# A four-layer conv and mixture-of-experts kernel: the wide layers' preparations issued tile by tile in the other half's expert stage, and their loops written out

## The chip, the cores and the metric

The kernel runs on one core of a Trainium2 chip. The metric is device time in microseconds. TensorE (PE) does the matmuls, VectorE (DVE), ScalarE (ACT) and GpSimd (POOL) the rest, SyncE (SP) issues plain DMAs and GpSimd the indirect ones. Each engine runs its own queue of instructions in order and waits on semaphores that other engines and DMAs raise.

## The reference

The input is 16 images of 64 channels and 24 x 24 pixels. Four blocks follow each other; each is a "conv" part and a "ffn" part, both added to their input:

```python
for l in range(4):
    x = x + conv[l](layernorm_over_channels(x))       # eps 1e-6
    t = tokens(x)                                      # 9216 tokens of 64
    t = t + ffn[l](layernorm(t))                       # eps 1e-5
    x = images(t)
# conv[0]: gate from the matrix square root (5 Newton-Schulz steps) of each image's covariance
# conv[1]: max over 2 of a*x + b, a and b from the pooled image;  conv[2]: gate from Haar band means
# conv[3]: 3 x 3 depthwise convolution and bias
# ffn[0], ffn[1]: 8 experts, 64 -> 128 (256) -> 64 with gelu and biases, the 2 best per token, weighted
# ffn[2], ffn[3]:
probs = softmax(flat @ router.T); p, idx = top_k(probs, 2); p = p / (p.sum() + 1e-9)
y = (silu(flat @ w1[e].T) * (flat @ w3[e].T)) @ w2[e].T     # 64 -> 682 -> 64, 8 experts
out = sum over the token's two experts of p * y
```

## The kernel before, in words

The images are worked on in two halves of 8 images, 4608 tokens each: `x[h]` holds 36 blocks of 128 tokens. Layers 0 and 1 are "narrow": every token goes through all 8 experts (`dense`), in slots of 512 tokens times one chunk of an expert, with the gates as factors. Layers 2 and 3 are "wide": tokens are sorted by expert. The order of the whole program is written by hand, each engine's queue for itself.

`prep(l, h)` is a half's preparation for a layer: layer norm (`ln`), the conv part, layer norm, routing (`route`). It is a generator with numbered steps (LN1, CONV, LN2, ROUTE), one on each engine; `Woven(prep(...)).upto(stage)` issues steps up to a number. In the narrow layers `dense` gets the other half's next preparation as `aside` and issues a few steps after each slot, by the plan of `weave`. For the wide layers the order is: `Woven(prep(2, 1)).upto(LAST)` alone, `moe(2, 0)`, `moe(2, 1)`, then `prep(3, 0)` and `prep(3, 1)` alone, the rounding of layer 3's weights (`wprep`), `moe(3, 0)`, `moe(3, 1)`, and the two last sums.

`moe(l, h)` is the expert stage of a half: 44 tiles (`TILES`) of 256 rows, 4 to a loop body (`UNROLL`), so 11 bodies (`LOOPS`); the first and the last are written out and the nine in between are a loop on each engine (`middle`). A tile's experts come from a packed word that TensorE loads per body (`experts`). Per tile TensorE transposes the rows of the tile after next (`turn_rows`, L1549, into banks 6 and 7 in turn), and for each of three groups (g) of hidden units does `up23` (8 matmuls, L1563 and L1564) and the last tile's `down23` (L1577, L1579). ScalarE does SiLU (`silu`, L753), a rounding (`high`, L761) and the copy of the transposed rows (`take`, L769, L770). DVE does `product` (L1189), `low` (L1193) and one `evict` (L1180) per tile.

Rows travel through DRAM. When `route` has the positions (`pos_ready`), GpSimd sends each of 36 blocks twice to its sorted places (`scatter`, `send`, L564, 72 indirect DMAs a half, reading `rowsb`). SyncE loads sorted tiles (L491) once all sends of the half have landed. GpSimd returns each finished tile with two indirect DMAs (`back`, L586) to token order; SyncE brings these back (`bring`, L523), and DVE's `combine` (L840 to L844) adds them to `x`. GpSimd's `back(l, 0, scatter(l, 1))` spreads the 72 sends of the second half over the 44 tiles of the first half's stage; `back(l, 1, ...)` has none beside it, and the sends of `scatter(3, 0)` follow the stages of layer 2 and lie beside `prep(3, 1)`.

SyncE loads the wide layers' weights in five pieces (`load_stage`, L479), ScalarE and DVE split each into two 16-bit parts. The expert output bias of the narrow layers is added on TensorE by two matmuls per unit with one row each (L1514). `conv0` forms each image's column sums (L1332) and covariance (L1340) image by image.

## Time and profile before

| | us |
|---|---|
| median of 3 runs | 2542.31 (2541.0 to 2554.62) |
| profiled execution | 2537.53 |
| its span, first to last instruction | 2535.7 |

| engine | busy us | share of the span |
|---|---|---|
| PE | 1678.8 | 66% |
| DVE | 1733.9 | 68% |
| ACT | 1347.7 | 53% |
| POOL | 980.1 | 39% |

The mean granted clock of TensorE is 0.778 of full speed. Times within the span are counted from its start. Busy times of an engine sum its instructions, which overlap a little on DVE and ACT. "Idle before" a row is the time in which the engine did nothing ahead of it, with what ended it; "issue" is a wait that nothing in the profile explains, "remote" one ended by no instruction that the profile could name.

### The profile page before, as it was taken

Reading aid. Unit: us, or ns where it says so; the run is one execution under the profiler, and the core shown is the slowest. Engines: PE = TensorE matmul, PEld = TensorE weight load, DVE = VectorE, ACT = ScalarE, POOL = GpSimd, SP = SyncE. Lnnn points to the kernel's source line nnn. Section 1 sums busy time; section 2 is a strip of 40 time slices with the busy share of each in tenths; the row PEclk is TensorE's granted clock in tenths of the full one; section 3 lists DMA queues with packets and bytes.
Section 4 is the critical chain, followed back from the end, with each engine's and each line's share of the span. In section 5 each row is a group of like instructions: output and inputs, shape, how many; then the busy total and the mean of one; then the engine's idle time right before and its main releaser. Section 6 shows DMA issues by size and latency. Waiting matters only on the chain.

```text
span 2535.7 us, 52266 instructions
## 1 busy us (share of the span) xinstructions
PE 1678.8 (66%) x17212; PEld 1245.9 (49%) x17213; DVE 1733.9 (68%) x2890; ACT 1347.7 (53%) x2453; POOL 980.1 (39%) x955
## 2 busy tenths in 40 slices
PE   4387787787867776537766679951221777777995
PEld 4253443453434433326666568840111666666884
DVE  3668668768775874566555568888775655556888
ACT  1356556777786677425445467740002544445774
POOL 1034334322231248404554534430481444553553
PEclk7587767878885879758788789975555877788998
DMA  6000000000020000000000020010002000002002
GB/s 276 22 2 1 23 1 1 1 2 1 2 85 5 1 9 21 15 4 26 25 24 23 17 65 26 27 66 0 12 22 78 26 24 23 24 18 63 27 27 82
DMA packets 52976, 75.98 MB, mean 30 GB/s; under 512 B 14873, under 2 KB 37610, under 8 KB 50174
## 3 DMA queue, kind: packets, MB, share of 16 engines
q1 hardware_dynamic: 30626, 43.26, 5.3%
q0 software_dynamic: 22208, 30.81, 3.5%
q8 instruction: 91, 1.49, 0.3%
q14 instruction: 51, 0.42, 0.1%
HBM read 40.89 MB, written 35.19 MB: 30 GB/s over the span
## 4 chain that ended last, share of the span: by engine, by line
PE 32%; DVE 14%; issue 7%; POOL 4%; ACT 4%; another core or an unknown queue 4%; DMA 1%; ACTq 0%; POOLq 0%; SPq 0%; DVEq 0%
PE bank L1563 11%; PE bank L1564 10%; PE bank L1577 4%; POOL rows L564 3%; DVE tmp L1030 2%; PE bank L1579 2%; POOL x L599 1%; DVE hb L1189 1%; ACT hl L761 1%; DVE act L1189 1%; PE bank L1459 1%; PE bank L1322 1%; ACT act L753 1%; ACT hb L753 1%
## 5 line engine op out<-in xcount | busy, mean ns | idle before, releaser
L586 POOL DMA_INDIRECT y<-ysb,ids x352 | 394.3, 1120 | 563.6 <-DVE ysb L1180 475.1
L599 POOL TENSOR_TENSOR x<-x,ysb 128x256 f32<-128x256 f32 x288 | 268.7, 933 | 668.6 <-DVE ysb L1258 660.6
L1563 PE MATMUL bank<-xT,gA 128*114 128x256 f16 x1056 | 342.3, 324 | 156.2 <-issue 51.3
L736 ACT ACTIVATE hb<-bank,bias_sb 128x512 f32<-128x512 f32 x432 | 298.8, 692 | 245.1 <-issue 137.1
L564 POOL DMA_INDIRECT rows<-rowsb,pos x288 | 305.4, 1060 | 293.8 <-DVE pos L1132 211.9
L1189 DVE TENSOR_TENSOR act<-bank,act 114x512 f32<-114x512 f32 x352 | 242.8, 690 | 236.5 <-ACT act L753 159.4
L753 ACT ACTIVATE act<-bank 114x512 f32<-114x512 f32 x352 | 210.2, 597 | 308.7 <-PE bank L1564 240.8
L1564 PE MATMUL bank<-xT,gB 128*114 128x256 f16 x1056 | 311.5, 295 | 0.0
L1563 PE MATMUL bank<-xT,uA 128*114 128x256 f16 x1056 | 311.2, 295 | 0.0
L1564 PE MATMUL bank<-xT,uB 128*114 128x256 f16 x1056 | 310.8, 294 | 0.0
L1577 PE MATMUL bank<-dW,hl 114*128 x2112 | 279.3, 230 | 32.2 <-issue 22.4
L1579 PE MATMUL bank<-dW,hl 114*128 x2112 | 260.8, 201 | 13.6 <-issue 13.3
L1563 PEld LDWEIGHTS bank<-xT,gA 128*114 x1056 | 148.6, 141 | 206.1 <-issue 194.2
L1193 DVE TENSOR_TENSOR hl<-act,hl 114x512 f16<-114x512 f32 x352 | 240.4, 683 | 0.0
L1577 PEld LDWEIGHTS bank<-dW,hl 114*128 114x128 f16 x2112 | 199.7, 103 | 59.5 <-issue 46.3
L761 ACT ACTIVATE hl<-act 114x512 f16<-114x512 f32 x352 | 220.6, 627 | 0.0
L1189 DVE TENSOR_TENSOR hb<-bank,hb 114x512 f32<-114x512 f32 x176 | 121.6, 691 | 131.9 <-ACT hb L753 96.2
L1579 PEld LDWEIGHTS bank<-dW,hl 114*128 114x128 f16 x2112 | 199.6, 103 | 16.6 <-issue 12.0
L1249 DVE TENSOR_TENSOR act<-hb,act 128x512 f16<-128x512 f32 x216 | 165.8, 768 | 49.0 <-ACT act L736 46.1
L1503 PE MATMUL bank<-rowsb,w 128*128 128x512 f16 x432 | 194.1, 449 | 6.2 <-DVE w0d L1238 6.2
L1249 DVE TENSOR_TENSOR hl<-hb,hl 128x512 f16<-128x512 f32 x216 | 159.3, 738 | 55.4 <-ACT hl L736 52.5
L1504 PE MATMUL bank<-rowsb,w 128*128 128x512 f16 x432 | 195.2, 452 | 0.0
(239 smaller groups left out, 3457.6 us busy)
## 6 DMA issues: line engine op xcount, KB each, us to landing
xs<-rows SPq DMA_DIRECT2D x176, 65.0 KB
stage<-up SPq DMA_DIRECT2D x8, 1368.0 KB, 6.1
rows<-land POOLq DMA_DIRECT2D x8, 1137.5 KB, 18.4
y<-ysb,ids POOLq DMA_INDIRECT x352
rows<-rowsb,pos POOLq DMA_INDIRECT x288
stage<-down SPq DMA_DIRECT2D x2, 1368.0 KB
rowsb<-y SPq DMA_DIRECT2D x4, 640.0 KB, 5.9
rows<-land POOLq DMA_DIRECT2D x4, 585.0 KB, 20.5
```

What stands on the lines that cost most here:

```text
L564: pool.indirect_dma_start(rows_d[l - SPARSE][h], bass.IndirectOffsetOnAxis(pos[h][:, k, j:j + 1], 0), words(h)[:, j * RW // 2:(j + 1) * RW ...
L586: pool.indirect_dma_start(y_d[h], bass.IndirectOffsetOnAxis(ids[h][:, t * SUB + u:t * SUB + u + 1], 0), ysb[t % UNROLL][:, u * C:(u + 1) * ...
L599: pool.tensor_tensor(xv, xv, tg[u % 2], ALU.add).then_inc(s["added"], 1)
L736: ins = a.activation(dst[:, 0:SPAN * P], PB[w % 3][:, :], ACT.Gelu, scale=1.0 / WSCALE, bias=b1T[l][:, at:at + 1])
L753: a.activation(hold(k, g)[0:CH, :], PB[q % 2][0:CH, :], ACT.Silu, scale=1.0 / WSCALE).then_inc(s["s_ready"], 1)
L761: a.activation(hl[g][0:CH, 0:2 * ROWS], hold(k, g)[0:CH, :], ACT.Copy).then_inc(s["hi_ready"], 1)
L1189: v.tensor_tensor(p, PB[2 + q % 2][0:CH, :], p, ALU.mult).then_inc(s["prod_ready"], 1)
L1249: v.tensor_tensor(p[:, SPAN * P:2 * SPAN * P], hid[w % 2][:, 0:SPAN * P], p[:, 0:SPAN * P], ALU.subtract).then_inc(s["lo_ready"], 1)
L1563: pe.matmul(PB[bank][0:CH, o], w[0][:, at], xT[k][:, :], start=True, stop=False)
L1564: ins = pe.matmul(PB[bank][0:CH, o], w[1][:, at], xT[k][:, :], start=False, stop=True)
L1577: pe.matmul(y[:, o:o + 2 * C], hl[g][0:CH, col:col + P], w, start=(g == 0 and c == 0 and u == 0), stop=False, skip_group_check=True)
L1579: ins = pe.matmul(y[:, o:o + C], hl[g][0:CH, 2 * ROWS + col:2 * ROWS + col + P], w[:, 0:C], start=False, stop=(g == G - 1 and c == 1), ski ...
```

## The change

Loops: `JOIN` and `middle` go; all 11 bodies of each stage are written out on TensorE, ScalarE and DVE (SyncE keeps its loop). Preparations: `moe` takes an `aside`, and after each of its 132 slots (44 tiles x 3) issues steps by the plan of `inner(l, h)`. `prep(2, 1)` is issued in `moe(2, 0)` from tile 1, `prep(3, 0)` in `moe(2, 1)` and `prep(3, 1)` in `moe(3, 0)` from tile 5, each over 48 slots (`INNER` 16 tiles); the combine of layer 3's first half is issued in `moe(3, 1)` from tile 5. Sends: GpSimd starts the sends beside a stage a tile before that plan ends (`inner_end`) and spreads the 72 over the tiles left; `scatter(3, 0)` now lies beside `back(2, 1)`. Banks: the transposed rows use bank 6 alone, since bank 7 (`BP`) serves the preparations. Narrow layers: the bias matmuls become one with two rows per unit (`b2p`, its second row moved there by a DMA), and `conv0` works on pairs of images with 128 columns.

```diff
-JOIN = 1
+INNER = 16
...
+            sp.wait_ge(s["stage_used"], 1)
+            sp.dma_start(b2p[1:2, :], b2[:, 2 * E * C:4 * E * C]).then_inc(s["b2_moved"], 16)
...
+        NSLOT = TILES * G
+
+        def inner(l, h):
+
+            if (l, h) == (NL - 1, 1):
+                todo, begin, over = [LN1 + k / 4 for k in range(8)], 5 * G, 8 * G
+            else:
+                l2 = (n_of(l, h) + 1) // HALVES
+                todo, begin, over = stages(l2), (G if l2 == SPARSE else 5 * G), INNER * G
+            return [-1] * begin + [todo[min(len(todo), -(-(v + 1) * len(todo) // over)) - 1] for v in range(NSLOT - begin)]
+
+        def inner_end(l, h):
+
+            plan = inner(l, h)
+            return plan.index(plan[-1]) // G
...
             def back(l, h, aside):
 
-                todo = TOPK * NT
+                todo, begin = TOPK * NT, inner_end(l, h) - 1
+                left = TILES - begin
                 for t in range(TILES):
-                    for _ in range((t + 1) * todo // TILES - t * todo // TILES):
+                    k = t - begin
+                    for _ in range((k + 1) * todo // left - k * todo // left if k >= 0 else 0):
                         next(aside, None)
...
                 back(l, 0, scatter(l, 1))
-                back(l, 1, iter(()))
-                if l + 1 < NL:
-                    first = scatter(l + 1, 0)
+                first = scatter(l + 1, 0) if l + 1 < NL else iter(())
+                back(l, 1, first)
...
-                    a.activation(xT[r][:, :], PB[6 + r % 2][:, :].bitcast(FP16)[:, 0:ROWS], ACT.Copy
+                    a.activation(xT[r][:, :], PB[6][:, :].bitcast(FP16)[:, 0:ROWS], ACT.Copy
                                  ).then_inc(s["xT_done"], 1)
...
-            Woven(prep(2, 1)).upto(LAST)
             for h in range(HALVES):
-                moe(2, h)
-            for h in range(HALVES):
-                Woven(prep(3, h)).upto(LAST)
+                moe(2, h, Woven(after(2, h)))
             Woven(wprep()).upto(LAST)
             for h in range(HALVES):
-                moe(3, h)
-            for h in range(HALVES):
-                for p in range(NP):
-                    combine(NL - 1, h, p)
+                moe(3, h, Woven(after(3, h)))
+            Woven(joined(NL - 1, 1)).upto(LAST)
...
-                        for i, b in enumerate((b2h[l], b2l[l])):
-                            row = b[:, e * C:(e + 1) * C].unsqueeze(1).broadcast_to([1, SPAN, C])
-                            pe.matmul(y[:, 0:SPAN * C], one16[0:1, :], row, start=(i == 0), stop=False, skip_group_check=True)
+                        row = b2p[:, (l * E + e) * C:(l * E + e + 1) * C].unsqueeze(1).broadcast_to([2, SPAN, C])
+                        pe.matmul(y[:, 0:SPAN * C], one16[0:2, :], row, start=True, stop=False, skip_group_check=True)
...
-                    if t == 0 or isinstance(i, int):
-                        wait_from(pe, s["xT_done"], i * UNROLL + (tb + k + t - 1))
-                    bank = PB[6 + r % 2][:, :].bitcast(FP16)
+                    wait_from(pe, s["xT_done"], i * UNROLL + (tb + k + t))
+                    bank = PB[6][:, :].bitcast(FP16)
...
+                            aside.upto(plan[(i * UNROLL + k) * G + g])
...
-                pe.wait_ge(s["route_ready"], 2 * (l + 1))
+                pe.wait_ge(s["route_ready"], n_of(l, h) + 1)
+                if (l, h) == (SPARSE, 0):
+                    pe.wait_ge(s["gated"], unit_base(SPARSE, 0))
                 turn_rows(0, 0, 0)
                 turn_rows(0, 1, 0)
-                body23(0, first=True)
-                middle(pe, body23)
-                body23(LOOPS - 1, last=True)
+                for i in range(LOOPS):
+                    body23(i, i == 0, i == LOOPS - 1)
+                aside.upto(LAST)
```

## Rows read from the trace of the kernel before

**Rows 1.** Busy time by stretch: start:end, length, PE, PEld, DVE, ACT, POOL, clock, DMA.

```profile
0.00:1048.00 1048.00, 749.76 (x8118) 424.78 (x8119) 718.61 (x1234) 657.62 (x1000) 352.94 (x381) 0.78 0.08 28
1048.00:1133.00 85.00, 27.09 (x114) 23.21 (x114) 56.42 (x110) 13.91 (x18) 1.66 (x2) 0.50 0.01 2
1133.00:1462.00 329.00, 230.45 (x2196) 207.56 (x2196) 182.37 (x308) 161.77 (x352) 160.46 (x156) 0.81 0.08 23
1462.00:1682.00 220.00, 193.46 (x2200) 171.25 (x2200) 182.31 (x309) 159.40 (x352) 103.97 (x90) 0.97 0.12 36
1682.00:1806.00 124.00, 24.01 (x92) 17.41 (x92) 97.78 (x148) 10.50 (x11) 6.77 (x6) 0.50 0.08 31
1806.00:1928.00 122.00, 24.02 (x92) 17.42 (x92) 96.28 (x148) 15.25 (x13) 84.42 (x73) 0.50 0.07 20
1928.00:1960.00 32.00, 0.31 (x4) 0.32 (x4) 14.88 (x5) 7.73 (x3) 0.00 (x0) 0.50 0.38 140
1960.00:2290.00 330.00, 236.08 (x2199) 211.83 (x2197) 181.93 (x308) 161.84 (x353) 160.43 (x156) 0.80 0.08 23
2290.00:2509.00 219.00, 193.52 (x2200) 172.16 (x2200) 181.52 (x307) 159.64 (x352) 104.46 (x89) 0.97 0.12 36
2509.00:2536.00 27.00, 0.05 (x2) 0.00 (x0) 21.79 (x17) 0.00 (x0) 4.95 (x4) 0.54 0.49 175
```

**Rows 2.** Timeline of DVE in layer 2's expert stages: start, us, line, tile.

```profile
1224.69 0.42 DVE L1180 TENSOR_REDUCE ysb<-bank 128x128 f32<-128x256 f32 x1
...
1393.31 0.42 DVE L1180 TENSOR_REDUCE ysb<-bank 128x128 f32<-128x256 f32 x1
...
1473.43 0.69 DVE L1189 TENSOR_TENSOR act<-bank,act 114x512 f32<-114x512 f32 x1 [12.32 <-ACT act L753]
...
1535.91 0.42 DVE L1180 TENSOR_REDUCE ysb<-bank 128x128 f32<-128x256 f32 x1
...
1639.67 0.42 DVE L1180 TENSOR_REDUCE ysb<-bank 128x128 f32<-128x256 f32 x1
```

**Rows 3.** Groups of GpSimd by line, 1133 to 1462 us: count, busy, mean ns, idle before.

```profile
L586 POOL DMA_INDIRECT y<-ysb,ids x85 | 89.9, 1058 | 149.5 <-DVE ysb L1180 120.2 <-issue 29.3
L564 POOL DMA_INDIRECT rows<-rowsb,pos x69 | 70.1, 1015 | 21.0 <-issue 20.7 <-POOL rowsb L572 0.3
```

**Rows 4.** Timeline of a run of GpSimd's calls and of TensorE and ScalarE beside it.

```profile
1434.50 0.27 PE L1564 MATMUL bank<-xT,uB 128*114 128x256 f16 x1
...
1435.10 1.01 POOL L586 DMA_INDIRECT y<-ysb,ids  x1 [0.30 <-issue]
...
1438.99 0.96 POOL L564 DMA_INDIRECT rows<-rowsb,pos  x1 [0.30 <-issue]
...
1441.37 0.60 ACT L753 ACTIVATE hb<-bank 114x512 f32<-114x512 f32 x1 [5.76 <-remote]
```

**Rows 5.** Waits of ScalarE, 1133:1460 (two rows) and 1465:1684: total, times, longest.

```profile
ACT hb L753 <- remote: 41.7, 9, 6.6
ACT act L753 <- remote: 22.8, 9, 5.3
...
ACT act L753 <- PE bank L1564: 37.8, 77, 2.4
```

**Rows 6.** Timeline of DVE in layer 1's second half: slots 1, 61 and 85.

```profile
766.96 0.69 DVE L1249 TENSOR_TENSOR hl<-hb,hl 128x512 f16<-128x512 f32 x1 [1.73 <-ACT hl L736]
...
913.76 0.69 DVE L1249 TENSOR_TENSOR hl<-hb,hl 128x512 f16<-128x512 f32 x1 [0.45 <-ACT hl L736]
...
946.33 0.68 DVE L1249 TENSOR_TENSOR hl<-hb,hl 128x512 f16<-128x512 f32 x1
```

**Rows 7.** Timeline of DVE in the tail: its wait for the second half's return.

```profile
2521.48 1.23 DVE L840 SCALAR_TENSOR_TENSOR rowsb<-rowsb,gts 128x1024 f32<-128x1024 f32 x1 [1.12 <-DMA xn<-y]
```

**Rows 8.** Timeline of SyncE after layer 2: loads of layer 3's weights.

```profile
1697.20 236.65 SPq L479 DMA_DIRECT2D stage<-up  x3
```

**Rows 9.** Timeline around a tile's start: ScalarE's copy, TensorE's first matmul.

```profile
1406.50 0.38 ACT L770 ACTIVATE xT<-bank 128x256 f16<-128x256 f16 x1
...
1407.04 0.31 PE L1563 MATMUL bank<-xT,gA 128*114 128x256 f16 x1 [0.70 <-DVE act L1189]
```

**Rows 10.** TensorE's bias matmuls of the narrow layers (line L1514), ns min/median/max.

```profile
L1514 PE MATMUL bank<-land,one x576: 267/278/416, 121.6 to 1043.7; 1*128 1x256 f16 x192
```

**Rows 11.** Timeline of DVE in the first layer: its wait for the column sums.

```profile
28.43 0.68 DVE L919 COPY gx<-bank 1x512 f32<-1x512 f32 x1 [7.04 <-PE bank L1332]
```

More of the change, by code:

```diff
@@ L378, in stages @@
         def stages(l):
-            return ([LN1 + k for k in range(10)] + [CONV + k for k in range(CONV_STEPS[l])] + [LN2 + k for k in range(10)]
+            first = [LN1 + k / 4 for k in range(8)] + [LN1 + k for k in range(2, 10)]
+            return ((first if l > SPARSE else [LN1 + k for k in range(10)]) + [CONV + k for k in range(CONV_STEPS[l])] + [LN2 + k for k in range(10)]
                     + [ROUTE + k for k in range(26)])
@@ L403, in experts @@
             return {k: eng.snap((w >> (3 * (k + 1))) & (E - 1), min_val=0, max_val=E - 1) for k in tiles}
-        def middle(eng, body):
-            with eng.Fori(0, (LOOPS - 2) // JOIN) as i:
-                for j in range(JOIN):
-                    body(i * JOIN + (j + 1))
         def split_base(l, h):
@@ L784, in body @@
                                 take(i, k, 2)
+                            aside.upto(plan[(i * UNROLL + k) * G + g])
                     if last:
                         high(i, UNROLL - 1, G - 1)
+                if (l, h) == (SPARSE, 0):
+                    a.wait_ge(s["down_ps"], slot_base(1, 1) + len(slots(1)))
                 take(0, 0, 0)
                 take(0, 1, 0)
-                body(0, first=True)
-                middle(a, body)
-                body(LOOPS - 1, last=True)
+                for i in range(LOOPS):
+                    body(i, i == 0, i == LOOPS - 1)
+                aside.upto(LAST)
             def after(l, h):
+                if (l, h) == (NL - 1, 1):
+                    return
                 yield from prep(*divmod(n_of(l, h) + 1, HALVES))
@@ L1207, in body23 @@
                                 low(i - 1, UNROLL - 1, G - 1)
-                            if k >= 2:
+                            if g == 0 and k >= 2:
                                 evict(i, k - 2)
-                            elif not first:
+                            elif g == 0 and not first:
                                 evict(i - 1, k + UNROLL - 2)
-                body23(0, first=True)
-                middle(v, body23)
-                body23(LOOPS - 1)
+                            aside.upto(plan[(i * UNROLL + k) * G + g])
+                if (l, h) == (SPARSE, 0):
+                    v.wait_ge(s["added"], unit_base(SPARSE, 0))
+                for i in range(LOOPS):
+                    body23(i, i == 0)
+                aside.upto(LAST)
                 low(LOOPS - 1, UNROLL - 1, G - 1)
@@ L1267, in dense, with joined @@
                 aside.upto(LAST)
+            def joined(l, h):
+                for p in range(NP):
+                    yield LN1 + p
+                    yield from combine(l, h, p)
             def after(l, h):
+                if (l, h) == (NL - 1, 1):
+                    yield from joined(NL - 1, 0)
+                    return
                 yield from prep(*divmod(n_of(l, h) + 1, HALVES))
@@ L1328, in conv0 @@
                 pe.wait_ge(s["mixed_ready"], turn(s["mixed_ready"]))
-                for smp in range(HB):
-                    ops = pieces(*divmod(smp, QS))
-                    for i, o in enumerate(ops):
-                        ins = pe.matmul(BP[0:1, smp * C:(smp + 1) * C], onef[:, 0:1], o, start=(i == 0), stop=(i == 4))
+                for s4 in range(QS):
+                    for i, o in enumerate(pieces(s4)):
+                        ins = pe.matmul(BP[0:1, s4 * P:(s4 + 1) * P], onef[:, 0:1], o, start=(i == 0), stop=(i == 4))
                 ins.then_inc(s["sums_ps"], 1)
@@ L1335, in conv0 @@
                 pe.wait_ge(s["rows_ready"], turn(s["rows_ready"]))
-                for smp in range(HB):
-                    q, s4 = divmod(smp, QS)
-                    ops = pieces(q, s4)
-                    for i, o in enumerate(ops):
-                        pe.matmul(BP[q * C:(q + 1) * C, s4 * C:(s4 + 1) * C], o, o, start=(i == 0 and s4 == 0),
-                                  stop=False, skip_group_check=True)
-                for smp in range(HB):
-                    q, s4 = divmod(smp, QS)
-                    ins = pe.matmul(BP[q * C:(q + 1) * C, s4 * C:(s4 + 1) * C], srow[0:1, 1, smp * C:(smp + 1) * C],
-                                    srow[0:1, 0, smp * C:(smp + 1) * C], start=False, stop=True, skip_group_check=True)
+                for s4 in range(QS):
+                    o4 = slice(s4 * P, (s4 + 1) * P)
+                    for i, o in enumerate(pieces(s4)):
+                        pe.matmul(BP[:, o4], o, o, start=(i == 0), stop=False, skip_group_check=True)
+                    ins = pe.matmul(BP[:, o4], srow[0:1, 1, o4], srow[0:1, 0, o4], start=False, stop=True, skip_group_check=True)
                 ins.then_inc(s["cov_ps"], 1)
@@ L1594, in body23 @@
                                 down23(i - 1, UNROLL - 1, g, es[-1])
+                            aside.upto(plan[(i * UNROLL + k) * G + g])
                     if last:
@@ L1618, in after @@
             def after(l, h):
+                if (l, h) == (NL - 1, 1):
+                    return
                 yield from prep(*divmod(n_of(l, h) + 1, HALVES))
@@ L1628, in _ @@
                     dense(l, h, Woven(after(l, h)))
[L1629 to L1637 removed]
+            for l in range(SPARSE, NL):
+                pe.wait_ge(s["w_lo"], (l - SPARSE + 1) * PIECES)
+                for h in range(HALVES):
+                    moe(l, h, Woven(after(l, h)))
 def kernel(**inputs):
```

56 lines of the change are left out of this document (28 added, 28 removed).

## The prediction

> **What bounds the kernel now.** I read three views in this order: busy time by stretch, the DVE's evictions (one per tile of 256 rows) and the waits of ScalarE. The stretches [rows 1] cut the 2535.7 us span into the two narrow layers (0 to 1048), the preparation of layer 2's second half (85 us), the expert stages of layer 2 (329 and 220 us), both preparations of layer 3 (124 and 122 us), the rounding of its weights (32 us), its expert stages (330 and 219 us) and 27 us of tail. Two things are to be seen.
>
> First, the three bare preparations (331 us) and the tail leave TensorE almost unused, but not VectorE: it is busy for 56.4 of 85, 97.8 of 124 and 96.3 of 122 us. A second-half expert stage has DVE busy for 182.3 of 220 us, of which 12.32 us are the wait at its start [rows 2], so about 88% while tiles run. What is woven into an expert stage goes onto an engine that is nearly full there.
>
> Second, the same 44 tiles take 110 us more in a first half than in a second half, at 0.81 granted clock against 0.97. From tile 12 to tile 34 one takes (1393.31 - 1224.69) / 22 = 7.66 us in the first half and (1639.67 - 1535.91) / 22 = 4.72 us in the second [rows 2]. All that differs is GpSimd's queue: in a first half it has, beside two returns per tile (L586), the 72 + 72 / 44 = 1.64 sends per tile (L564) of the other half's rows, about 1.3 us each with the 0.30 us before them [rows 3]. GpSimd is only 49% busy, so its own time isn't the bound. What I see is TensorE's signals held back while GpSimd issues many calls in a row: the last matmul of a group (L1564) starts at 1434.50, GpSimd issues without a gap until 1439.95, and ScalarE's SiLU on that bank (L753) starts at 1441.37 after 5.76 us of idle time [rows 4]. Such waits come to 64.5 us in the first half; in the second, where calls come in twos, the longest of ScalarE's waits for that bank is 2.4 us [rows 5]. So a first half is bound by runs of GpSimd calls; a second half by DVE, with TensorE close behind.
>
> A rule speaks against that reading: the Trainium skill, page "SBUF — State Buffer", section "Who interferes with whom", says that PE and ACT never wait on anyone. The wait in this trace, 5.76 us, disagrees; what would follow if the rule held here is the first rival.
>
> **The change part by part.** Sums are against the profiled execution (2537.5 us, span 2535.7).
>
> *Sends.* The number of sends is the same, 144 per layer, but the 72 of layer 3's first half leave the bare preparation after it (84.4 us of GpSimd in 1806 to 1928 [rows 1], which cost nothing there) and enter the second expert stage of layer 2. So three expert stages carry them, not two. They are also denser: GpSimd starts them only a tile before the woven preparation ends, tile 15 of 44 in layer 2's first stage (72 sends in 29 tiles, 2.5 each) and tile 19 in the next two (72 in 25, 2.9 each). A tile then has 4.5 to 4.9 GpSimd calls in a row. Price: the first half of now pays 7.66 - 4.72 = 2.94 us per tile for 1.64 sends, 1.8 us per send by these rows, and by the stages 329 - 220 plus 8 us of shorter start = 117 us per 72 sends, 1.6 us each. In denser runs the start of a run, which isn't held, is shared: a tile of 4.1 us unheld work plus 0.9 us of landing plus 1.3 us for each call past the second gives 8.2 to 8.7 us, or 9.0 to 9.6 where two tiles' runs join, so 8.6 and 9.1 us; minus 4.72, that is 112 us a stage. Three stages 336 against 234 now: **+102**. Bounds: GpSimd's own time as the only limit (4.5 and 4.9 calls of 1.3 us, 5.8 and 6.4 us a tile: 31 + 2 x 42 = 115 in all, -119), and 1.8 us for each send (389, +155).
>
> *Preparations.* Each is issued in slots (three a tile), one or two steps after each slot's own work, over 16 tiles from tile 1 or tile 5. Nearest row: layer 1's second half, where layer 2's first preparation is woven into the first 65 slots. Its first 60 slots take 913.76 - 766.96 = 146.8 us, the 24 after them 32.6, 1.36 us each [rows 6]: weaving costs 146.8 - 60 x 1.36 = 65 us for work that stands bare at 85, though DVE has far more room there. Beside experts DVE is at 88%, so the floor is DVE's own time: 56.4 less some 8 us idle in 16 tiles for layer 2, 97 less 8 for layer 3. Above it come steps in which TensorE waits in order for DVE and DVE for TensorE. I take 78 us for layer 2's (bare 85: -7) and 114 for each of layer 3's (bare 124 and 122: -18). Bounds 48 to 90 and 88 to 140. The last two tiles of each lie beside sends, when DVE idles anyway: -6 and twice -10. Together **-51**. Behind the steps queue, on DVE the next product, on TensorE the next gate matmuls, on ScalarE the next SiLU; that is why I don't go to the floor.
>
> *Combine.* The sums of layer 3's first half, 11 us of DVE at 2509, go beside tiles of the last stage. The tail doesn't shorten, since DVE then waits for the second half's return at 2521.48 [rows 7] in any case. DVE in that stage gets 10.6 us more: **+7** (0 to +11).
>
> *Weights of layer 3.* SyncE's second load waits behind the return of layer 2's second half; it was issued at 1697.20 and done in the shade of a preparation [rows 8]. Now no preparation stands between, and the 32 us stretch begins with that return, about 6 us of returns and 6 of load: **+12** (+5 to +20).
>
> *One bank for transposed rows.* Bank 7 goes to the preparations, so the transposes of the tile after next wait for ScalarE's copy of the next one. TensorE starts a tile at 1407.04 when the product is there; the copy before runs at 1406.50 for 0.38 us [rows 9]. The transposes used to fit into the wait ahead; now they follow the copy, 0.2 to 0.4 us a tile where nothing else is late, the 44 tiles of the last stage and some 10 others: **+15** (0 to +50).
>
> *Loops written out.* The load of the expert word remains. Tiles inside a body take about 0.2 us less than the mean of 4.72, so a turn costs 0.8 us, nine per stage, and only the last stage runs unhindered: **-5** (0 to -30, all 36 turns). The Trainium skill, page "Runtime: NRT & Kernel Launch", section "Instruction fetch mechanics", says that a taken branch out of the current pages stalls for a fetch, while straight code is fetched ahead. By that rule the whole -30 would come; where a stage is held by GpSimd or DVE, a turn has nothing to give back.
>
> *Narrow layers.* One bias matmul per unit goes (288 of 576, 0.28 us each, overlapped [rows 10]), on TensorE's path only where it is last; DVE's wait for TensorE's column sums in the first layer (7.04 us [rows 11]) and the like shorten by 1 or 2 us, twice; a 2 us wait for the moved bias row is added at 118 us. TensorE is busy for 750 of 1048 us there: **-16** (0 to -40).
>
> Sum: +102 - 51 + 7 + 12 + 15 - 5 - 16 = **+64**, span 2600, time 2602; the median of the runs lies 4.8 us over the profiled execution, so **2605 us**.
>
> **The rivals.** *GpSimd's runs don't hold TensorE* when they are sends only or regular, as the sends issued back to back from 1806 to 1928 didn't lengthen that preparation (122 against 124 us [rows 1]). Against: the first half's tiles [rows 2]. Then sends cost 115 in all, not 336: 2605 - 221 = 2384. (The Trainium skill's rule of the SBUF page above would have this result.) *Weaving at the floor*: DVE never waits, and the bank costs nothing: preparations 48 and twice 88, combined -56 more, -15 for the bank, -10 elsewhere: about 2520. For: 88% in [rows 1]. Against: [rows 6]. *Sends at the full price*: 1.8 us for each (+53), and no shade for a preparation's last tiles (+26), because joined runs hold TensorE while DVE waits for it: about 2684, slower than now. It decides once a run of calls outlasts the work that lies ready, as ten calls of two joined tiles would (13 us). *The change hides nothing because steps pile up*: if GpSimd's wait for the positions at tile 15 or 19 blocks its returns, DVE's evictions stop four tiles later; I give it little, since the positions come in the same tile by the plan.
>
> **How the numbers follow.** Chances: my forecast (2550 to 2645) 0.42, full price (2645 to 2710) 0.13, weaving at the floor (2480 to 2550) 0.24, unheld TensorE (2330 to 2480) 0.17, piled-up steps (above 2710) 0.04. The range 2450 to 2680 holds about 8 in 10; the forecast's own is 2550 to 2645. A measurement of this kernel tells about 0.5% (13 us) from no change: faster 0.36, same 0.09, slower 0.55.
>
> **What would show it.** In the changed profile: the second stage of layer 2 at some 430 us with 72 sends in it, last tiles at 8.5 to 9.5 us with long ScalarE waits beside runs of five GpSimd calls, and a granted clock near 0.8; tiles with preparation at 9 (layer 2) and 11 to 12 us (layer 3) with DVE at 85% or more; the last stage at 225 to 235 us. I am wrong if tiles beside sends take 6 to 7 us, or if a woven preparation of layer 3 adds under 95 us.

## The result, and the profile after

The changed kernel takes 2650.07 us (median of 4 runs, 2647.22 to 2650.71), the kernel before beside it 2541.65 us: a ratio of 1.0427 (95% interval 1.0401 to 1.0452). It is slower by 108 us. The forecast was 2605 us, in a range from 2450 to 2680. The profiled execution took 2647.22 us with a span of 2645.3 us, against 2535.7 before, so 109.6 us have to be found.

Busy time by stretch, after (start:end, length, PE, PEld, DVE, ACT, POOL, clock, DMA). These answer to [rows 1]: the narrow layers; first stage of layer 2 with its preparation and then with sends; second stage, plain, with preparation, with sends; weights; the same three parts of layer 3's first stage; the last stage; the tail.

```profile
0.00:1041.00 1041.00, 708.77 (x7656) 411.71 (x7656) 720.33 (x1236) 655.69 (x1000) 352.27 (x381) 0.79 0.08 28
1041.00:1230.00 189.00, 124.24 (x1030) 114.75 (x1029) 129.26 (x236) 90.14 (x172) 40.09 (x36) 0.75 0.05 15
1230.00:1454.00 224.00, 145.28 (x1282) 129.41 (x1280) 108.03 (x183) 93.71 (x203) 120.91 (x121) 0.75 0.08 23
1454.00:1507.00 53.00, 33.76 (x316) 29.32 (x317) 34.62 (x51) 24.54 (x55) 15.10 (x15) 0.76 0.21 68
1507.00:1712.00 205.00, 119.12 (x933) 109.58 (x932) 155.15 (x258) 77.93 (x150) 44.49 (x41) 0.70 0.05 12
1712.00:1900.00 188.00, 119.86 (x1047) 106.26 (x1045) 88.11 (x149) 75.72 (x164) 106.14 (x107) 0.74 0.08 23
1900.00:1957.00 57.00, 5.02 (x24) 4.10 (x25) 16.08 (x6) 14.29 (x11) 9.22 (x8) 0.50 0.39 150
1957.00:1995.00 38.00, 28.55 (x294) 25.17 (x293) 33.88 (x49) 22.74 (x50) 9.00 (x8) 0.86 0.07 19
1995.00:2202.00 207.00, 123.23 (x943) 113.55 (x941) 152.71 (x257) 77.90 (x150) 46.01 (x42) 0.68 0.05 13
2202.00:2397.00 195.00, 115.72 (x1036) 102.90 (x1036) 87.92 (x149) 75.56 (x163) 109.71 (x110) 0.73 0.08 23
2397.00:2620.00 223.00, 196.75 (x2200) 172.84 (x2200) 189.26 (x317) 160.60 (x352) 98.06 (x87) 0.98 0.12 36
2620.00:2646.00 26.00, 0.00 (x0) 0.00 (x0) 10.69 (x8) 0.00 (x0) 3.92 (x4) 0.50 0.51 182
```

The ledger by place, in us. The middle columns are from [rows 1] and the rows above; "forecast" is the sum of the prediction's terms that fall into the place.

| place | before | after | change | forecast |
|---|---|---|---|---|
| narrow layers | 1048 | 1041 | -7 | -16 |
| layer 2: first stage and `prep(2, 1)` | 85 + 329 | 413 | -1 | -18 |
| layer 2: second stage and `prep(3, 0)` | 220 + 124 | 446 | +102 | +92 |
| weights of layer 3 | 32 | 57 | +25 | +12 |
| layer 3: first stage and `prep(3, 1)` | 122 + 330 | 440 | -12 | -23 |
| layer 3: last stage | 219 | 223 | +4 | +17 |
| tail | 27 | 25.3 | -1 | 0 |
| sum | | | +110 | +64 |

So nearly the whole loss stands in one place, the second stage of layer 2, where the sends of layer 3's first half were moved to, and no place gives more than 12 us back.

The evictions of after, one per tile (timeline of DVE; start, us): first stage tiles 1 and 17, second stage tiles 1, 5, 22 and 44, last stage tiles 20 and 38. [Rows 2] are their counterparts.

```profile
1062.39 0.42 DVE L1205 TENSOR_REDUCE ysb<-bank 128x128 f32<-128x256 f32 x1
...
1229.66 0.42 DVE L1205 TENSOR_REDUCE ysb<-bank 128x128 f32<-128x256 f32 x1
...
1478.39 0.42 DVE L1205 TENSOR_REDUCE ysb<-bank 128x128 f32<-128x256 f32 x1
...
1506.97 0.42 DVE L1205 TENSOR_REDUCE ysb<-bank 128x128 f32<-128x256 f32 x1
...
1712.23 0.42 DVE L1205 TENSOR_REDUCE ysb<-bank 128x128 f32<-128x256 f32 x1
...
1899.41 0.42 DVE L1205 TENSOR_REDUCE ysb<-bank 128x128 f32<-128x256 f32 x1 [2.25 <-remote]
...
2511.78 0.42 DVE L1205 TENSOR_REDUCE ysb<-bank 128x128 f32<-128x256 f32 x1
...
2596.73 0.42 DVE L1205 TENSOR_REDUCE ysb<-bank 128x128 f32<-128x256 f32 x1
```

Three paces are to be read there. With preparation a tile takes (1229.66 - 1062.39) / 16 = 10.45 us in layer 2's first stage and (1712.23 - 1506.97) / 17 = 12.07 us in the second; with sends (1899.41 - 1712.23) / 22 = 8.51 us; undisturbed (2596.73 - 2511.78) / 18 = 4.72 us, as before. The plain tile hasn't changed, everything else is an extra on it.

A run of GpSimd's calls in the send part and ScalarE beside it (timeline; idle time before in brackets), the counterpart of [rows 4]:

```profile
1804.45 1.00 POOL L601 DMA_INDIRECT y<-ysb,ids  x1 [1.09 <-DVE ysb L1205]
...
1809.58 0.95 POOL L577 DMA_INDIRECT rows<-rowsb,pos  x1 [0.30 <-issue]
...
1811.70 0.60 ACT L768 ACTIVATE hb<-bank 114x512 f32<-114x512 f32 x1 [4.36 <-remote]
```

Five calls follow each other from 1804.45 to 1810.53; ScalarE's SiLU starts 1.2 us after the last one, having waited 4.36 us. The forecast's picture, runs of five calls and long waits beside them, is there. Between tiles 22 and 44 of the second stage 103 calls come in 17 runs, 6.1 calls each.

### The profile page after: what moved, and what is told of

The parts are those of the page before. It is cut to its first block, busy times and chain, and to the rows that moved or that the text cites. A ratio compares the mean times of both kernels' runs of the same rounds, so it can differ in the third digit from the quotient of the medians.

```text
span 2645.3 us, 49395 instructions
## 1 busy us (share of the span) xinstructions
PE 1720.3 (65%) x16748; PEld 1319.6 (50%) x16748; DVE 1726.1 (65%) x2892; ACT 1368.8 (52%) x2466; POOL 954.9 (36%) x955
## 4 chain that ended last, share of the span: by engine, by line
PE 24%; DVE 18%; issue 10%; ACT 5%; another core or an unknown queue 5%; POOL 4%; DMA 1%; SPq 0%; POOLq 0%; ACTq 0%; DVEq 0%
PE bank L1588 8%; PE bank L1589 8%; POOL rows L577 3%; DVE hl L1218 3%; PE bank L1602 3%; DVE act L1214 3%; DVE tmp L1054 2%; ACT hl L776 2%; ACT act L768 1%; PE bank L1604 1%; DVE hb L1214 1%; PE bank L1574 1%; POOL x L614 1%; PE bank L1484 1%
## 5 line engine op out<-in xcount | busy, mean ns | idle before, releaser
L1588 PE MATMUL bank<-xT,gA 128*114 128x256 f16 x1056 | 360.5, 341 | 258.4 <-DVE act L1214 104.3
L1589 PE MATMUL bank<-xT,gB 128*114 128x256 f16 x1056 | 337.9, 320 | 0.0
L1588 PE MATMUL bank<-xT,uA 128*114 128x256 f16 x1056 | 336.4, 319 | 0.0
L1589 PE MATMUL bank<-xT,uB 128*114 128x256 f16 x1056 | 336.1, 318 | 0.0
L1602 PE MATMUL bank<-dW,hl 114*128 x2112 | 303.8, 242 | 39.0 <-issue 26.4
L577 POOL DMA_INDIRECT rows<-rowsb,pos x288 | 289.2, 1004 | 82.9 <-issue 74.8
L1588 PEld LDWEIGHTS bank<-xT,gA 128*114 x1056 | 163.2, 155 | 308.1 <-issue 299.7
L1604 PE MATMUL bank<-dW,hl 114*128 x2112 | 283.6, 210 | 19.4 <-issue 19.2
L1602 PEld LDWEIGHTS bank<-dW,hl 114*128 114x128 f16 x2112 | 220.4, 111 | 50.4 <-issue 41.7
L1604 PEld LDWEIGHTS bank<-dW,hl 114*128 114x128 f16 x2112 | 214.4, 108 | 30.2 <-issue 19.8
L768 ACT ACTIVATE hb<-bank 114x512 f32<-114x512 f32 x176 | 105.0, 597 | 231.5 <-remote 136.9
L1528 PE MATMUL bank<-rowsb,w 128*128 128x512 f16 x432 | 193.5, 448 | 7.9 <-DMA land<-land 7.9
```

The costliest lines, as they stand in the source:

```text
L577: pool.indirect_dma_start(rows_d[l - SPARSE][h], bass.IndirectOffsetOnAxis(pos[h][:, k, j:j + 1], 0), words(h)[:, j * RW // 2:(j + 1) * RW ...
L768: a.activation(hold(k, g)[0:CH, :], PB[q % 2][0:CH, :], ACT.Silu, scale=1.0 / WSCALE).then_inc(s["s_ready"], 1)
L1588: pe.matmul(PB[bank][0:CH, o], w[0][:, at], xT[k][:, :], start=True, stop=False)
L1589: ins = pe.matmul(PB[bank][0:CH, o], w[1][:, at], xT[k][:, :], start=False, stop=True)
L1602: pe.matmul(y[:, o:o + 2 * C], hl[g][0:CH, col:col + P], w, start=(g == 0 and c == 0 and u == 0), stop=False, skip_group_check=True)
L1604: ins = pe.matmul(y[:, o:o + C], hl[g][0:CH, 2 * ROWS + col:2 * ROWS + col + P], w[:, 0:C], start=False, stop=(g == G - 1 and c == 1), ski ...
```

## Experiments

Each ran beside the kernel before on its chip; the ratio is to that one. The medians of before differ by chip, so ratios are compared, not times: 2520.7 us beside the two kernels with sends behind DVE's products, the written-out bodies and the one bank; 2542.6 beside the gated kernel of before, the two kernels with sends in rows and the narrow layers alone; 2546.9 beside the last four (bare preparation, gated calls in the changed kernel, weights first, combined).

### Sends behind DVE's products, on the kernel before

```diff
-                    for _ in range((t + 1) * todo // TILES - t * todo // TILES):
-                        next(aside, None)
                     pool.wait_ge(s["y_done"], tile_base(l, h) + t + 1)
...
+                    calls = (t + 1) * todo // TILES - t * todo // TILES
+                    for c in range(calls if h == 0 else 0):
+                        pool.wait_ge(s["prod_ready"], group_base(l, h) + min((t + 2) * G + 2 + c * 2 // calls, TILES * G))
+                        next(aside, None)
```

> The kernel before, with the same 72 sends beside each first-half stage, but never in a long run: after a tile's two returns GpSimd waits for the product of the next slot before it issues a send, and for the one after it before the second send, so that at most two calls follow each other. Theory (runs of three and more calls hold TensorE's signals): a tile with sends falls from 7.66 us to about 6.0 us, the two first-half stages from 330 to about 260 us, in all -140 (2400 us; -100 to -200). Rival 1 (the number of calls, GpSimd's busy time or the traffic of the sends sets the price, not how they are grouped): 7.6 us a tile, 2540 us +-10. Rival 2 (every call holds signals for its own length, however it is placed): calls now meet every slot, a tile stays at 7.7 to 8.5 us, 2540 to 2600 us.

Measured: 0.9983 (0.9964 to 1.0002), no difference that counts. The edit didn't do what it was for. GpSimd's timeline shows why:

```profile
1308.33 1.35 POOL L584 DMA_INDIRECT y<-ysb,ids  x1 [2.08 <-DVE ysb L1182]
...
1316.91 0.96 POOL L564 DMA_INDIRECT rows<-rowsb,pos  x1 [0.30 <-issue]
```

Seven calls in a row, of which the first and the last are shown: two tiles' returns with two sends between and one behind. The product waited for was already made when GpSimd came to the wait, so the wait ended nothing. The experiment can't tell the theory from its rival, since the runs were still there.

### The same sends in the changed kernel

The same edit, with the changed kernel's own count of sends per tile.

> The changed kernel, with the sends placed as in the first kernel of this batch: after a tile's two returns one or two sends behind the wait for the next slot's product, one more behind the wait for the slot after it; number and stages of the sends as in the changed kernel (2.5 to 2.9 a tile). Theory (long runs hold TensorE's signals): tiles beside sends fall from 8.3 to 9.1 us to GpSimd's own time, 4.5 to 4.9 calls of 1.3 us and a little more, about 6.5 us: 71 tiles by 2.1 us, -150, about 2500 us (2450 to 2550). Rival 1 (their number or traffic sets the price): 2650 us +-10. Rival 2 (DVE and TensorE lose the time in other waits of the woven order): under -50, 2600 us or more.

Measured: 1.0377 (1.0351 to 1.0404), some 12 us under the changed kernel. Its runs became only a little shorter: 4.7 calls each against 6.1 between tiles 22 and 44 of the second stage, at 7.90 us a tile against 8.51.

### Sends behind TensorE's own signal, on the kernel before

```diff
                     for u in range(SUB):
+                        if u > 0 and h == 0:
+                            pool.wait_ge(s["h_ps"], group_base(l, h) + min((t + 2) * G + 3, TILES * G))
                         pool.indirect_dma_start(y_d[h], ...
...
+                    for c in range(calls if h == 0 else 0):
+                        pool.wait_ge(s["h_ps"], group_base(l, h) + min((t + 3) * G + 1 + c, TILES * G))
+                        next(aside, None)
```

> The kernel before, with each of GpSimd's calls in a first-half stage after the first return of a tile behind a signal of TensorE itself: the second return waits for the gate and up matmuls two slots on, the sends for those of the next tile's first and second slot. The waits on products in the earlier kernel were already met when GpSimd was late, so its runs stayed at up to seven calls; a signal of TensorE isn't there while it is held, so here a run must end. Theory (a run of three and more calls is what holds TensorE's signals, one or two calls hold them little): runs of at most two or three, tiles of a first half from 7.3 to about 5.7 us, -140 us (-80 to -200) against before. Rival 1 (each call costs the same however placed): -20 us or less. Rival 2 (GpSimd waits too long, its returns come late and DVE waits for a free output buffer): slower than before.

Measured: **0.958** (0.9549 to 0.961), 107 us faster than before with the same number of calls in the same stages. The two first-half stages, by stretch (columns as above):

```profile
1136.00:1408.00 272.00, 210.73 (x2192) 186.27 (x2190) 181.12 (x308) 158.25 (x349) 164.83 (x156) 0.92 0.10 27
1912.00:2190.00 278.00, 206.25 (x2200) 180.85 (x2200) 184.31 (x309) 160.20 (x354) 166.66 (x156) 0.94 0.10 27
```

272 and 278 us against 329 and 330 [rows 1], GpSimd busy for slightly more than before (165 and 167 against 160 us), the granted clock 0.92 and 0.94 against 0.81 and 0.80. Only the grouping of the calls differs. ScalarE's waits of the kind of [rows 5], ended by nothing that the profile names, fall from 64.5 us in the first stage to 13.5, 51 of the 57 us. Counted in the timelines between tiles 12 and 34 of the first stage (a run is a series of calls at most 0.35 us apart):

| kernel | calls | runs | calls per run | calls in runs of five or more | us per tile |
|---|---|---|---|---|---|
| before | 80 | 18 | 4.4 | 54% | 7.66 |
| behind DVE's products | 80 | 25 | 3.2 | 48% | 6.96 |
| behind TensorE's signal | 81 | 34 | 2.4 | 12% | 6.14 |

The number of calls or their traffic as the whole price is thereby ruled out, and so is a fixed price for each call however placed. Of the 1.4 us that a gated tile still takes over the plain 4.72 no run says whether it belongs to the runs left or to the calls as such. The 6.96 us of the middle row come from another chip, on which the kernels with written-out bodies and with one bank, whose sends are as before, show 7.33 and 7.48, and that kernel as a whole was no faster (0.9983): it isn't a gain that counts. I had expected 5.7 us a tile; runs of three were still frequent (15 of 34).

### All sends in one row, on the kernel before

```diff
-                back(l, 0, scatter(l, 1))
+                for _ in scatter(l, 1):
+                    pass
+                back(l, 0, iter(()))
```

> The kernel before, with the 72 sends of each second half issued in one row as soon as its positions are there, ahead of the first half's returns, and none between the returns. 72 calls take 84 us. Theory (sends beside tiles cost TensorE's signals): from the point where they are out, tiles take 4.7 us instead of 7.3; the first-half stages lose 110 us each, and pay 84 us of sends less what the first four or five tiles and the 32 us of layer 3's weights cover: -80 to -130 us against before. While the sends run, a tile should take 10 us or more, since TensorE's signals come one by one. Rival 1 (a first half is slower for another reason, such as the lower clock or the second-half rows' traffic): tiles stay above 6 us after the sends, 0 to +100 us. Rival 2 (TensorE isn't held by a row of sends alone): the first tiles take 4.7 us until the output buffers are full.

Measured: 0.9614 (0.9585 to 0.9644), 98 us faster. The row of 72 calls runs from 1134.4 to 1225.5. ScalarE's timeline in it, with one row of DVE's and some of TensorE's:

```profile
1145.52 0.27 PE L1566 MATMUL bank<-xT,uB 128*114 128x256 f16 x1
...
1151.37 0.60 ACT L755 ACTIVATE hb<-bank 114x512 f32<-114x512 f32 x1 [7.11 <-remote]
...
1151.99 0.69 DVE L1191 TENSOR_TENSOR hb<-bank,hb 114x512 f32<-114x512 f32 x1 [7.30 <-issue]
...
1152.83 0.46 PE L1565 MATMUL bank<-xT,gA 128*114 128x256 f16 x1 [6.69 <-issue]
...
1154.36 0.42 PE L1566 MATMUL bank<-xT,uB 128*114 128x256 f16 x1
...
1175.21 0.60 ACT L755 ACTIVATE act<-bank 114x512 f32<-114x512 f32 x1 [22.73 <-remote]
...
1182.91 0.21 PE L1581 MATMUL bank<-dW,hl 114*128 x1 [1.84 <-issue]
...
1185.70 0.27 PE L1579 MATMUL bank<-dW,hl 114*128 x1 [2.58 <-issue]
...
1220.01 0.60 ACT L755 ACTIVATE act<-bank 114x512 f32<-114x512 f32 x1 [43.69 <-remote]
```

This is the plainest view of the mechanism. ScalarE reads the banks in the order in which TensorE fills them. The three SiLUs shown are the stage's third, fourth and fifth; the groups of matmuls that they read ended at about 1142.8, 1145.8 (its last row starts at 1145.52) and 1154.8 (1154.36). The signals thus arrive some 9, 29 and 65 us late, and ScalarE idles for 7, 23 and 44 us. From there signals go at once: SiLU ends at 1151.97 and DVE's product starts at 1151.99; it ends at 1152.68 and TensorE's matmul starts at 1152.83.

TensorE itself is slow in the row, too. The eight matmuls of `down23` have one wait ahead of them in the kernel and none between, yet from 1180.80 on they start 2.1 to 2.8 us apart, each after idle time that nothing in the profile explains; elsewhere in the expert stages such a group takes under 1 us. Between the signals read at 1175.21 and at 1220.01 lie 16 matmuls, (1220.01 - 1175.21) / 16 = 2.8 us each. By these rows, and as an estimate, it looks as if what TensorE has finished were let go one instruction after another while GpSimd issues calls; TensorE runs ahead until it can't any more, then keeps the same step. No experiment tested this reading. The lateness outlasts the row: ScalarE's next SiLU starts at 1235.52 after 14.03 us, 10 us after the last call, and the first tile is finished at 1238.6. My expected 10 us a tile was far too little: a row of sends stops the stage. After it the two first-half stages run like second-half ones; the rest of the first:

```profile
1236.00:1440.00 204.00, 185.12 (x2112) 165.27 (x2113) 176.07 (x299) 152.89 (x339) 99.79 (x86) 0.98 0.09 26
```

### All sends in rows, on the changed kernel

```diff
-                    for _ in range((k + 1) * todo // left - k * todo // left if k >= 0 else 0):
-                        next(aside, None)
```

The sends then follow the last return of each stage.

> The changed kernel, with the sends taken out from between the returns of all three stages and issued in one row after the stage's last return. Theory (the price of sends beside tiles, and the woven preparations at the price seen in the changed kernel): the last 28, 22 and 22 tiles of the three stages go from 8.3 to 8.5 us to 4.7, -266; three rows of 84 us come, one of them beside 57 us of weights, +200; together -65 us against the changed kernel (-30 to -100). Tiles with preparation stay at 10.4 (layer 2) and 12.1 us (layer 3), since they had almost no sends beside them. Rival (tiles late in a stage are slow since steps of the woven order or the clock hold them): they stay at 6 us or more, and the kernel gets slower by 50 to 150 us.

Measured: 1.0179 (1.0147 to 1.0212), 63 us under the changed kernel; the rival is out, since the late tiles fall to the plain pace, as the rows show (second stage, tiles 22 and 44; then tile 1 of the third stage):

```profile
1696.41 0.42 DVE L1203 TENSOR_REDUCE ysb<-bank 128x128 f32<-128x256 f32 x1
...
1795.12 0.42 DVE L1203 TENSOR_REDUCE ysb<-bank 128x128 f32<-128x256 f32 x1 [0.64 <-PE bank L1602]
...
1922.24 0.42 DVE L1203 TENSOR_REDUCE ysb<-bank 128x128 f32<-128x256 f32 x1
```

(1795.12 - 1696.41) / 22 = 4.49 us. Tiles 22 to 44 of the undisturbed second stage of before take the same, (1681.47 - 1582.67) / 22 = 4.49, since the last tiles of a stage are quicker than 4.72. The sum came out right by luck in part: the tiles that had carried sends shrank by 285 us in all where I expected 266, and the way from one stage's last eviction to the next one's first grew by 90 and by 99 us at the two rows of sends with no weights beside them, where I put 84 a row.

### The same, and layer 3's first preparation bare

```diff
             for h in range(HALVES):
-                moe(2, h, Woven(after(2, h)))
+                moe(2, h, Woven(after(2, 0) if h == 0 else iter(())))
+            Woven(after(2, 1)).upto(LAST)
```

(on TensorE, ScalarE and DVE)

> The changed kernel with its sends in bare rows (the last experiment on it), and in addition the preparation of layer 3's first half taken out of the second expert stage and issued bare behind it, as in the kernel before. Against that last experiment (ratio 1.018 to before). Theory (a woven preparation costs what it costs bare: 17 tiles by 12.1 - 4.7 us = 125 us against a bare 124 us): no change, 1.015 +-0.004. Prediction's step (114 us woven): slower by 10 us, 1.022. Rival (weaving reaches VectorE's own time, 88 us): slower by 35 us, 1.032.

Measured: 1.0137 (1.0097 to 1.0178), so 0.4% below the 1.0179 with the preparation woven (measured on another chip, each against its own before). The intervals overlap; no gain from weaving is to be seen, and a gain of 35 us is excluded. In the traces the second stage, first eviction to last, shrinks from 326.6 us (1468.52 to 1795.12) to 197.5 us, and the way to the next stage's first eviction grows from 127.1 to 245.3 us:

```profile
1473.95 0.42 DVE L1204 TENSOR_REDUCE ysb<-bank 128x128 f32<-128x256 f32 x1
...
1671.47 0.42 DVE L1204 TENSOR_REDUCE ysb<-bank 128x128 f32<-128x256 f32 x1 [0.38 <-PE bank L1604]
...
1916.74 0.42 DVE L1204 TENSOR_REDUCE ysb<-bank 128x128 f32<-128x256 f32 x1
```

Woven, the preparation costs 129 us; bare, 118. Hidden beside 44 tiles it is no cheaper than alone.

### One change at a time: loops, bank, narrow layers

Written out: `middle` becomes a plain Python loop over the nine bodies.

> The kernel before, with all eleven bodies of each expert stage written out on TensorE, ScalarE and DVE, nothing else. Prediction's step: -5 us (0 to -30) on the four stages, most of it in the two second-half stages. Rival (a turn of the loop costs a fetch of code on every engine, 0.8 us each, 36 turns): -30 us. Rival (written-out code has to be fetched and falls behind): slower by 10 us or more.

Measured: 0.9926 (0.9885 to 0.9968), 19 us (8 to 29), between my 5 and the rival's 30 us. Second stage, tiles 12 and 34:

```profile
1519.27 0.42 DVE L1179 TENSOR_REDUCE ysb<-bank 128x128 f32<-128x256 f32 x1
...
1620.85 0.42 DVE L1179 TENSOR_REDUCE ysb<-bank 128x128 f32<-128x256 f32 x1
```

4.62 us a tile against 4.72 [rows 2], 0.4 us a turn. The rule of the Trainium skill that the prediction weighed here ("Runtime: NRT & Kernel Launch", "Instruction fetch mechanics") had the right direction; my own -5 was too small. Whether the 0.4 us are a fetch or something else of the turn these rows don't tell.

One bank: `PB[6 + r % 2]` becomes `PB[6]`, TensorE waits for the next tile's copy.

> The kernel before, with the transposed rows in bank 6 alone and TensorE's wait for the copy of the next tile, nothing else. Prediction's step: 0.2 to 0.4 us for each of the 88 tiles of the second-half stages, +18 to +35 us here (+15 in the changed kernel). Rival (the transposes fit beside the wait for DVE in any case; the changed kernel's last stage has the same 4.72 us a tile): 0 to +5 us.

Measured: 1.0051 (1.0018 to 1.0083), 13 us (5 to 21). A tile takes (1632.14 - 1526.70) / 22 = 4.79 us, 0.08 more, a quarter of what I took per tile.

```profile
1526.70 0.42 DVE L1180 TENSOR_REDUCE ysb<-bank 128x128 f32<-128x256 f32 x1
...
1632.14 0.42 DVE L1180 TENSOR_REDUCE ysb<-bank 128x128 f32<-128x256 f32 x1
```

Narrow layers: the parts of the diff for `b2p`, `pieces` and `conv0` alone.

> The kernel before, with the changes in the narrow layers alone: one bias matmul of two rows in place of two, the moved bias row, and column sums and covariance for pairs of images. Prediction's step: -16 us (0 to -40) in the first 1048 us. From the changed kernel's trace, whose narrow part ends 7 us earlier: -7 us (-3 to -12). The experts' stages stay as they are.

Measured: 0.9987 (0.9968 to 1.0007), 3 us; not to be told from nothing.

### Gated calls in the changed kernel

The gates of the third experiment, in the tiles that carry sends; a third send of a tile follows the second return.

> The changed kernel with GpSimd's calls behind signals of TensorE in the tiles that carry sends, as in the gated kernel of before, at most two calls without a wait by the plan. Number and stages of the sends are unchanged, 2.5 to 2.9 a tile. Theory (the runs' length sets the hold; gated, a send cost (5.97 - 4.72) / 1.64 = 0.76 us): tiles beside sends from 8.5 to about 6.8 us, 71 tiles, -117 us against the changed kernel: about 0.997 of before (0.985 to 1.012). Rival (at 4.9 calls a tile GpSimd is too full for gaps): under -50 us, 1.023 or more.

Measured: 1.0063 (1.004 to 1.0086), 93 us under the changed kernel. Between tiles 22 and 44 of the second stage a tile takes 7.53 us with 3.9 calls a run, against 8.51 with 6.1; I had expected 6.8. With five calls a tile three gates per tile aren't enough to keep runs short (65% of the calls are in runs of five or more).

### Layer 3's second weight piece first

```diff
                 if l == 3:
-                    load_stage(3, range(1, PIECES))
+                    load_stage(3, range(2, PIECES))
...
+                if l == 2:
+                    load_stage(3, range(1, 2))
                 bring(l, 1)
```

> The changed kernel, with SyncE's load of the second piece of layer 3's weights issued ahead of the return of layer 2's second half, not behind it. Theory (the load stands behind that return and ScalarE waits 21.6 us for it): 57 us of weights fall to 38 to 45, ratio to before from 1.043 to 1.037 (-12 to -20 us). Rival (the returns' own traffic, or the third piece, is what is late): 1.041 or more.

Measured: 1.0405 (1.0361 to 1.0449), not to be told from the changed kernel's 1.0427. The trace sides with the rival. In the changed kernel ScalarE waited for the second piece (timelines of SyncE and ScalarE):

```profile
1912.61 0.33 SPq L536 DMA_DIRECT2D rowsb<-y  x1
...
1914.41 15.36 SPq L490 DMA_DIRECT2D stage<-up  x3
...
1923.90 2.48 ACT L721 ACTIVATE gA<-stage 128x2736 f16<-128x2736 f32 x1 [21.55 <-DMA stage<-up]
```

In this one the second piece is there, and it waits as long for the third, which now stands behind the return:

```profile
1931.61 2.48 ACT L723 ACTIVATE uA<-stage 128x2736 f16<-128x2736 f32 x1 [21.04 <-DMA stage<-up]
```

### The useful parts together

Before, with gated calls, written-out bodies and the narrow layers' changes; preparations bare, two banks, and 26 of the 72 sends of layer 3's second half issued while its weights are rounded:

```diff
+                if (l, h) == (NL - 1, 0):
+                    for _ in range(EARLY):
+                        next(aside)
+                    todo -= EARLY
```

> The kernel before with the gated calls, the expert stages' bodies written out, the narrow layers' changes, and 26 of the 72 sends of layer 3's second half issued in one row while layer 3's weights are rounded and TensorE has nothing to do; preparations bare, two banks for the transposed rows, as before. Sum of the single ratios: 0.958 - 0.007 - 0.001, and 26 sends that no longer stand beside tiles, 0.76 us each, -20 us or 0.008: 0.942 of before, about 2390 us (2370 to 2410). Rival (the effects share their gain, since a gated stage isn't bound by DVE): 0.95.

Measured: 2397.42 us, **0.9404** (0.9367 to 0.9441): faster than both kernels, by 6% than the one before and by 10% than the changed one (0.9404 / 1.0427 = 0.902). The effects add up as single ones. Layer 3's first stage, with 1.05 sends a tile left:

```profile
1905.00:2158.00 253.00, 201.65 (x2200) 180.40 (x2200) 186.23 (x309) 160.58 (x353) 142.29 (x140) 0.94 0.11 29
```

## Why the prediction was right in direction and 45 us short

**TensorE's signals and the sends.** Right, and now shown. The forecast's first rival, that runs of calls don't hold TensorE, is out by the gated kernel and by the row of 72. The rule of the Trainium skill that was weighed there ("SBUF — State Buffer", "Who interferes with whom") says TensorE never waits on anyone. The section speaks of access to SBUF. This case's trace shows TensorE's signals up to 65 us late, and matmuls 2.1 to 2.8 us apart with no wait between them in the kernel; whether access to SBUF has a part in it no run here shows. The size was a little high: 8.28 to 8.83 us a tile beside sends, not 8.6 to 9.1. The 4.1 us of unheld work and 0.9 us of landing in the forecast's formula stood on no row; the fixed 1.3 us for each call past the second came near, though the row of 72 shows that the hold isn't a fixed time per call. Over the plain 4.72 us that makes 96, 83 and 90 us for the three stages, 270 in all, where I had 336 less 26 of shade. A first half before paid (1460.69 - 1146.58) - 43 x 4.72 = 111 us, twice:

```profile
1146.58 0.42 DVE L1180 TENSOR_REDUCE ysb<-bank 128x128 f32<-128x256 f32 x1
...
1460.69 0.42 DVE L1180 TENSOR_REDUCE ysb<-bank 128x128 f32<-128x256 f32 x1 [0.66 <-PE bank L1579]
```

So sends cost +47 us net, where the forecast had +102, or +76 with its 26 us of shade. (Against the same tiles of an undisturbed stage, whose last tiles are quicker, it is 285 less 233, +52.)

**Preparations.** This is the step that failed. I took 78, 114 and 114 us, 25 us less than the bare 331. Measured over the plain pace they cost 100, 135 and 137 us, 371 in all, 40 **more** than bare. (Per stage: the tiles from 1 to 17, or from 1 to 22, less 4.72 us each; and 8 us for a late first tile in the first stage, 1062.39 - 1041 against 1146.58 - 1133.) For layer 3 DVE's own time is 97 less 8 us; I put 25 us on top, and it took 46 and 48. What the sum left out is to be read in the waits in the second stage's preparation part, 1507 to 1712: DVE's, then TensorE's (total us, times, longest):

```profile
DVE act L1214 <- ACT act L768: 33.6, 13, 9.2
DVE hb L1214 <- ACT hb L768: 8.7, 8, 2.0
```

```profile
PE bank L1588 <- DVE act L1214: 30.6, 10, 7.7
...
PE bank L1353 <- DVE tmp L1032: 10.8, 7, 2.5
...
PE bank L1489 <- DVE mt L1104: 7.1, 1, 7.1
```

DVE is busy for 155 of 205 us, 76%, where the forecast said 85% or more and the floor would have it full. Where a step needs TensorE and DVE in turn, TensorE waits in its queue for DVE's step (L1353, L1489), the next slot's gate and up matmuls stand behind it, ScalarE's SiLU and DVE's product behind those: 42 us of DVE's waits. The forecast named this queueing and gave it too few us; the bare-preparation experiment confirms the total (129 against 118). Not tried was how much the clock has to do with it: it stood at 0.70 and 0.68 in the two parts with layer 3's preparations, against 0.97 in an undisturbed stage, and slower matmuls lengthen the same chain.

**Taken together**, sends and preparations came to +87 us, where I had +51: 29 too high in one, 65 too low in the other. That the whole sum was off by no more than 45 us is in part luck of this kind. The place ledger hides this, since the border between the two parts isn't sharp.

**Weights of layer 3.** Right mechanism, +25 for +12. I put 6 us for the return and 6 for the load. From the last eviction to the issue of the return 13 us pass (1912.61 - 1899.41), as in the kernel before (1695.40 - 1681.47 = 14), where a preparation lay beside them; from the issue of the load to ScalarE's rounding it takes another 9.5 us (1923.90 - 1914.41). Both are longer than the 6 us that I gave them. The row of before:

```profile
1695.40 0.33 SPq L523 DMA_DIRECT2D rowsb<-y  x1
```

**Last stage.** +4 instead of +17. The combine is as forecast: it is the only thing that slows tiles there (DVE busy for 189.3 us against 181.5; first to last eviction 206.3 us against 197.7). The place shows less, since the wait ahead of its first eviction is 6 us shorter (16.7 against 22.8). The bank's cost (0.08 us a tile) and the written-out loop's gain (0.10) cancel, in agreement with the unchanged pace of 4.72 us. Both sizes were wrong, the one 3 to 4 times too large, the other too small, and the sum of the two was +10 where it is about 0.

**Narrow layers.** -7 in the trace and 3 us in the runs of that part alone, instead of -16: TensorE's busy time fell by 41 us (749.8 to 708.8), but hardly any of it stood on the path.

## What to carry to other kernels

Work woven into a stage in which one engine is 88% busy and three engines hand over to each other in turn wasn't hidden here: price it at its bare time until a trace shows less. Look at runs of GpSimd's indirect DMAs before anything else: keep them to one or two by waiting between them for a signal of the engine that they hold, since a wait for another engine's signal may long be met. A gate holds a run short only if there are enough of them for the calls of a tile. Moving such calls from a bare stretch, where they cost nothing, into a busy one has to be paid for by what the move makes room for.

## What the runs showed of the hardware

- While GpSimd issues indirect DMAs one after another (0.96 us each, 0.30 us apart), signals of TensorE reach ScalarE late: ScalarE waits 4 to 7 us beside runs of four to eight calls. In a row of 72 the signals come some 9, 29 and 65 us after the matmuls, with waits of 7.11, 22.73 and 43.69 us, and matmuls with no wait between them start 2.1 to 2.8 us apart. ScalarE's and DVE's signals arrive within 0.02 and 0.15 us in the same stretch. Which path is shared wasn't found: no run here looked at it, and whether GpSimd's computing operations have the effect wasn't tried.
- Ending the runs also raised TensorE's granted clock in those stages, from 0.81 and 0.80 to 0.92 and 0.94 of full speed; TensorE was idle there for 61 us of 272 against 99 us of 329.
- A turn of a four-tile loop on three engines costs 0.4 us in a stage whose DVE is 88% busy (4.62 us a tile written out, 4.72 in the loop).
